# A convolution in far and near parts, and a 1x1 output product as three float32r products

## The reference

```python
xn = group_norm(x)                                  # 32 groups, no scale or shift
f  = relu(Wc @ xn + bc)                             # 1x1, 256 -> 64 channels
g  = relu(mean_hw(xn) @ Wc.T + bc)                  # 64 values
g_kern = g * Wkk + bkk                              # 64 x 3 x 3
sk = relu(Wc @ max_over_3x3_blocks(xn) + bc)        # 64 x 3 x 3
dynW = relu(Wck[:, 0] * g_kern + Wck[:, 1] * sk + bck)   # out 64 x in 64 x 3 x 3
y  = conv3x3(f, dynW, pad=1) + b_ad                 # another kernel for each image
out = x + Wf @ y + bf                               # 1x1, 64 -> 256 channels
```

## Time and profile before

| | |
|---|---|
| time, median of 3 runs | 511.19 us |
| lowest, highest | 509.42, 512.63 us |
| span of the profiled execution | 507.5 us |
| PE, PEld busy | 487.8, 383.7 us |
| DVE, ACT, POOL busy | 418.9, 426.6, 296.2 us |
| DMA | 158.01 MB, 311 GB/s |

### The profile page before, as it was taken

How to read it: one execution, slowest core, us unless ns; L and a number is a source line. 1 busy time by engine, 2 the same in 40 slices (tenths; PEclk the granted TensorE clock), 3 DMA queues, 4 the chain that set the end, 5 groups by cost and what they waited for, 6 DMA issues and landing times.

```text
span 507.5 us, 19231 instructions
## 1 busy us (share of the span) xinstructions
PE 487.8 (96%) x8349; PEld 383.7 (76%) x8349; DVE 418.9 (83%) x653; ACT 426.6 (84%) x486; POOL 296.2 (58%) x231
## 2 busy tenths in 40 slices
PE   5989999999999999999999999999999999999993
PEld 2454664677788888888888978888887878888781
DVE  6978879988888889888888988888889887888544
ACT  5779999998999999999999899999999989995231
POOL 5224586555577655556775555577655556765543
PEclk9999999999999999999999999999999999999997
DMA  8945778999898998998999999989999998953467
GB/s 335 418 134 201 265 283 289 366 353 349 323 333 334 323 332 340 348 359 293 320 362 333 333 365 343 318 297 360 307 366 334 341 333 298 361 208 145 185 270 296
DMA packets 48868, 158.01 MB, mean 311 GB/s; under 512 B 4752, under 2 KB 15888, under 8 KB 48784
## 3 DMA queue, kind: packets, MB, share of 16 engines
q1 hardware_dynamic: 34096, 93.07, 54.0%
q10 hardware_dynamic: 14688, 63.70, 31.0%
HBM read 75.94 MB, written 75.50 MB: 298 GB/s over the span
## 4 chain that ended last, share of the span: by engine, by line
PE 81%; ACT 2%; DVE 0%; issue 0%; DVEq 0%; ACTq 0%
PE ps L1129 30%; PE ps L1260 23%; PE ps L1228 21%; PE ps L1179 7%; ACT unused L609 1%; DVE X L859 0%; ACT unused L596 0%; ACT f_hi L688 0%; DVEq L153 0%; ACT f L694 0%; ACT Y L586 0%; PE ps L1372 0%; ACT dyn_b L709 0%; ACT dyn_hi L707 0%; ACTq L130 0%
## 5 line engine op out<-in xcount | busy, mean ns | idle before, releaser
L859 DVE SCALAR_TENSOR_TENSOR X<-ps,out_bias,X 128x960 f32<-128x960 f32 (+1 forms) x189 | 185.2, 1008 | 17.1 <-PE ps L1260 16.8
L1260 PE MATMUL ps<-Y,const 64*64 64x480 f32 (+1 forms) x1536 | 165.1, 486 | 0.0
L596 ACT ACTIVATE unused<-X,neg_mean 128x2304 bf16<-128x2304 f32 x60 | 132.0, 2201 | 0.4 <-DVE neg_mean L998 0.4
L512 POOL TENSOR_TENSOR dyn_a<-const,pool_g 128x576 f32<-128x576 f32 x30 | 34.9, 1165 | 163.8 <-DVE pool_g L883 163.8
L609 ACT ACTIVATE unused<-X 128x2304 bf16<-128x2304 f32 x60 | 126.9, 2115 | 0.0
L1228 PE MATMUL ps<-X,wcn_t 64*64 64x384 f32 (+1 forms) x1296 | 115.5, 486 | 0.7 <-issue 0.7
L935 DVE TENSOR_REDUCE feats<-X 128x6 f32<-128x1536 f32 x64 | 111.6, 1744 | 0.0
L1228 PEld LDWEIGHTS ps<-X,wcn_t 64*64 64x64 f32 x1296 | 82.0, 133 | 29.8 <-issue 7.4
L1260 PEld LDWEIGHTS ps<-Y,const 64*64 64x64 f32 x1536 | 78.2, 133 | 7.5 <-issue 2.8
L527 POOL TENSOR_TENSOR f_lo<-f,f_hi 128x1152 f16<-128x1152 f32 x32 | 71.4, 2232 | 19.5 <-ACT f L694 19.5
L1129 PE MATMUL ps<-f_hi,dyn_hi 64*64 64x480 f16 x1152 | 69.0, 365 | 2.5 <-ACT dyn_hi L715 1.1
(11 more groups left out here) (101 smaller groups left out, 541.8 us busy)
## 6 DMA issues: line engine op xcount, KB each, us to landing
X<-x SPq DMA_DIRECT2D x63, 1152.0 KB, 9.5
out<-X ACTq DMA_DIRECT2D x54, 1152.0 KB, 9.7
out<-X SPq DMA_DIRECT2D x7, 1152.0 KB, 8.0
out<-X SPq DMA_DIRECT2D x6, 480.0 KB, 3.5
stack<-f_hi SPq DMA_DIRECT2D x64, 32.5 KB, 2.5
stack<-f_lo SPq DMA_DIRECT2D x64, 32.5 KB, 5.4
X<-x SPq DMA_DIRECT2D x2, 576.0 KB, 7.1
upper<-f_hi SPq DMA_DIRECT2D x32, 32.5 KB, 3.5
```

Source lines behind the costliest of these rows:

```text
L596: nc.scalar.activation(unused[:, t], pixels(u, t), ACT.Square, scale=1.0 / SIDE, bias=neg_mean[:, n % 2, 1:2], accum_out=feats[:, (n + 1) ...
L859: nc.vector.scalar_tensor_tensor(out=out, in0=unit_psum(piece, bank, col), scalar=out_bias[:, t:t + 1], in1=out, op0=ALU.add, op1=ALU.add) ...
L1260: mm = nc.tensor.matmul(ps[rows, bank + q, col:col + width], wft[lanes, t, rows], Y[lanes, n % 2, at:at + width], start=True, stop=True)
```

## The change

The convolution no longer has a rest with stacked rows. Each block of 24 rows is done as 7 + 7 far rows and 5 + 5 near rows, near and far from the seam between the blocks: `conv(n, FAR, term)` has products of 336 columns, `conv(n, NEAR, term)` of 240, both three terms of 36 products of 64*64. One row on each side of the seam is copied by DMA (`halo`) instead of five rows three or two times.

y leaves PSUM as two float32r tensors: ACT writes the rounded Y_hi, DVE writes Y_lo as the difference. The output weights are split the same way once. A unit is three float32r products (hi x hi, hi weights x lo, lo weights x hi), each for both blocks, with 64 rows and 128 columns of the array (64*128). `project_f` is the 128*64 form in every image, now 512, 512 and 139 columns wide. The gains move from DVE to ACT, the rounding of the dynamic weights from ACT to POOL, two Newton steps from DVE to POOL, and all stores from ACT's queue to SP's. PSUM banks are dealt anew, and all lists of calls are in another order.

```diff
--- before.py
+++ after.py
...
-MAIN_ROWS = 10
-MAIN = MAIN_ROWS * SIDE
-REST_ROWS = HROWS - 2 * MAIN_ROWS
-REST = REST_ROWS * SIDE
-STACK_ROWS = 2 * (REST_ROWS + 1)
...
+FAR, NEAR = 0, 1
+ROWS = (7, 5)
+PART = tuple(rows * SIDE for rows in ROWS)
+FIRST = (((0, 7), (10, 17)), ((14, 19), (0, 5)))
...
+NEAR_BANK = 4
+NEAR_AT = 256
...
+CHUNKS = ((0, 512), (512, 512), (1024, 128))
...
+OUT_UNITS = ((0, 0), (0, 1), (1, 0), (1, 1), (0, 2), (1, 2))
+UNITS = len(OUT_UNITS)
+PIECES = ((0, PART[FAR]), (PART[FAR], PART[FAR]), (2 * PART[FAR], PART[NEAR]))
+UNIT_BANKS = (2, 6, 6, 6, 2, 6)
+PENULT_BANKS = (2, 6, 2, 6, 2, 6)
+LAST_BANKS = (2, 6, 0, 2, 6, 0)
+PENULT_AIDED = (5,)
...
+            def halo(f, ready, arrived, n):
+                if inside(n):
+                    sp.wait_ge(*ready)
+                    sp.dma_start(f[CM:P, n % 2, 0:1, :], f[0:CM, n % 2, HROWS:HROWS + 1, :]) \
+                        .then_inc(arrived[n % 2], 16)
+                    sp.dma_start(f[0:CM, n % 2, HROWS + 1:HROWS + 2, :], f[CM:P, n % 2, 1:2, :]) \
+                        .then_inc(arrived[n % 2], 16)
...
+            for i in range(1, N - 1):
+                load(i + AHEAD, 0)
+                seam_low(i)
+                load(i + AHEAD, 1)
+                seam_high(i + 1)
+                store(i - 1, 0)
+                store(i - 1, 1)
...
+                nc.gpsimd.tensor_scalar(wf_hi[:], wft[:], 1.0, 1.0, ALU.mult, ALU.mult).then_inc(wf_step, 1)
+                pool.wait_ge(wf_step, 2)
+                nc.gpsimd.tensor_tensor(wf_lo[:], wft[:], wf_hi[:].bitcast(F32), ALU.subtract) \
...
+                nc.gpsimd.tensor_scalar(dyn_a[:], per_gain[:], mean_act[:, n % 2, MEAN:MEAN + 1], 1.0,
+                                        ALU.mult, ALU.mult).then_inc(dyn_step, 1)
...
+            def weights_high(n):
+                if inside(n):
+                    pool.wait_ge(dyn_step, count(n - SUMS, SUM_STEPS, SUM_STEPS))
+                    pool.wait_ge(conv_mm[NEAR], count(n, -1))
+                    nc.gpsimd.tensor_scalar(dyn_hi[:, n % 2], dyn_a[:], MOST, 0.0, ALU.min, ALU.max) \
+                        .then_inc(dyn_hi_ready, 1)
...
-            def y_main_out(n):
-                u, lap = n % RING, n // RING
-                if inside(n):
-                    act.wait_ge(main_mm, count(n, 1))
-                    nc.scalar.activation(Y[:, n % 2, 0:2 * MAIN].rearrange("p (b f) -> p b f", b=2),
-                                         ps[:, 0:2, 0:MAIN], ACT.Identity).then_inc(y_main, 1)
+                act.wait_ge(squares, halves_done(N - 1, 1))
...
+            def y_high_out(n, part):
+                if inside(n):
+                    act.wait_ge(conv_mm[part], count(n, 1))
+                    nc.scalar.activation(part_y(Y_hi, part), part_psum(part), ACT.Identity) \
+                        .then_inc(y_high[part], 1)
...
+                proj = ps_flat[:, HPIX:HPIX + FEATS]
+                nc.vector.tensor_scalar(f_bias[:, n % 2:n % 2 + 1], proj[:, NEG:NEG + 1], bcs[:], None, ALU.add)
+                nc.vector.tensor_scalar(mean_act[:, n % 2], proj[:, 0:TAPS + 1], bcs[:], 0.0,
+                                        ALU.add, ALU.max).then_inc(relu_ready, 1)
...
-            def y_rest_out(n):
-                u, lap = n % RING, n // RING
-                if inside(n):
-                    dve.wait_ge(rest_mm, count(n, 1))
-                    both = ps[:, rest_bank(n):rest_bank(n) + 2, 0:REST].rearrange("p q f -> p f q")
-                    nc.vector.tensor_reduce(Y[:, n % 2, 2 * MAIN:HPIX], both, AX.X, ALU.add).then_inc(y_rest, 1)
...
+            def y_low_out(n, part):
+                if inside(n):
+                    dve.wait_ge(conv_mm[part], count(n, 1))
+                    dve.wait_ge(y_high[part], count(n, 1))
+                    nc.vector.tensor_tensor(part_y(Y_lo, part), part_psum(part), part_y(Y_hi, part).bitcast(F32),
+                                            ALU.subtract).then_inc(y_low[part], 1)
...
+            def conv(n, part, term):
+                pe_terms = ((dyn_hi, f_hi), (dyn_lo, f_hi), (dyn_hi, f_lo))
+                order = (0, 2, 1) if n < SUMS else (0, 1, 2)
+                w, f = pe_terms[term]
                 if term == 0:
                     pe.wait_ge(f_evac, count(n, 1, 2))
                     pe.wait_ge(dyn_hi_ready, highs_done(n, 0))
...
+                    wait(pe, y_high[part], n)
+                    wait(pe, y_low[part], n)
+                    if part == NEAR:
+                        pe.wait_ge(halo_hi[n % 2], 32 * (n // 2 + 1))
+                        pe.wait_ge(f_evac, count(min(n + 2, N), 0, 2))
+                        ahead = 2 if n < EARLY else 3
+                        pe.wait_ge(var_ready, min(n + ahead, N))
+                        pe.wait_ge(neg_ready, min(n + ahead + 1, N))
+                elif term == 1:
...
+                        r = FIRST[part][q][h] + dy
+                        bank, at = (q, 0) if part == FAR else (NEAR_BANK + q, NEAR_AT)
                         mm = nc.tensor.matmul(
...
+                            ps[CM * h:CM * (h + 1), bank, at:at + PART[part]],
                             w[lanes, n % 2, tap, :],
...
+                at, width = CHUNKS[c]
+                column = at
+                if c == len(CHUNKS) - 1:
+                    wait(pe, y_low[NEAR], n, -1)
+                if c == len(CHUNKS) - 1 and n >= SUMS:
+                    width += FEATS
                     pe.wait_ge(feats_read, count(n, 1))
                 for t in range(HALVES):
                     for h in range(2):
...
+                        src = half(n % RING, t) + HPAD * h + at
+                        mm = nc.tensor.matmul(ps_flat[CM * h:CM * (h + 1), column:column + width],
+                                              wcn_t[:, n % 2, t, :], X[:, src:src + width],
                                               start=(t == 0), stop=(t == HALVES - 1))
                 mm.then_inc(f_mm, 1)
...
                 mm.then_inc(feats_mm, 1)
-            def product(n, k, t, piece, bank, col):
-                at, width, _ = PIECES[piece]
-                for q, h in ((0, 0), (1, 1), (0, 1), (1, 0)):
-                    lanes, rows = (slice(CM * tile, CM * (tile + 1)) for tile in (q, h))
-                    mm = nc.tensor.matmul(ps[rows, bank + q, col:col + width], wft[lanes, t, rows],
-                                          Y[lanes, n % 2, at:at + width],
-                                          start=True, stop=True)
+            terms = ((wf_hi, Y_hi), (wf_hi, Y_lo), (wf_lo, Y_hi))
+            def product(n, k):
+                t, piece = OUT_UNITS[k]
+                at, width = PIECES[piece]
+                bank = unit_bank(n, k)
+                for s, (w, y) in enumerate(terms):
+                    for h in range(2):
+                        lanes = slice(CM * h, CM * (h + 1))
+                        mm = nc.tensor.matmul(ps[:, bank + h, 0:width], w[lanes, t, :], y[lanes, at:at + width],
+                                              start=(s == 0), stop=(s == len(terms) - 1))
                 mm.then_inc(out_mm, 1)
+            def products_near(n):
...
+            def products_near(n):
+                for turn in range(2):
+                    for k in (4, 5):
+                        t, piece = OUT_UNITS[k]
+                        at, width = PIECES[piece]
+                        bank = unit_bank(n, k)
+                        for s, (w, y) in enumerate(terms):
+                            for h in range(2):
+                                lanes = slice(CM * h, CM * (h + 1))
+                                side = (turn + h) % 2
+                                if turn == 1 and s == 0:
+                                    pe.wait_ge(handed[1 - h], count(n, k - 3, 2))
+                                mm = nc.tensor.matmul(ps[:, bank + side, h * width:(h + 1) * width], w[lanes, t, :],
+                                                      y[lanes, at + side * width:at + (side + 1) * width],
+                                                      start=(s == 0), stop=(s == len(terms) - 1))
+                                if turn == 0 and s == len(terms) - 1:
+                                    mm.then_inc(handed[h], 1)
+                        if turn == 1:
+                            mm.then_inc(out_mm, 1)
             def unit(k, n):
...
+                conv(i, FAR, 0)
+                unit(1, i - 1)
+                if i > TURN:
+                    project_f(i + 1)
+                    unit(2, i - 1)
+                    conv(i, FAR, 1)
+                    group_sums(i + 2)
+                    unit(3, i - 1)
+                    conv(i, FAR, 2)
+                else:
                     if i < EARLY:
...
+                units_near(i - 1)
+                conv(i, NEAR, 0)
+                conv(i, NEAR, 2 if i < SUMS else 1)
+                conv(i, NEAR, 1 if i < SUMS else 2)
+                unit(0, i)
```

(66 more changed lines are left out.)

808 lines of the change are left out of this document (310 added, 498 removed).

## The result

The changed kernel takes **580.38 us** (median of 4 runs, 579.44 to 582.07) against 510.31 for the kernel before on the same chip (507.68 to 512.63). The ratio is 1.138, with a 95% interval of 1.133 to 1.143. The direction was forecast (chance 57%), the size was not: 536, with a range up to 551.

The account below looks back on a forecast made before the run. TensorE, full at 14.62 us an image, was taken as the bound: 13.9 plus 1.6 for ten form changes gives 15.5, +0.88 over 27 images, plus 1 for start and end, 536 us; own range 515 to 550, with rivals 496 to 551.

Parts of the forecast that it names:

- TensorE's own work: TensorE's list in a steady image: 13.9 us plus 1.6 for form changes, 15.5 against 14.62.
- A float32r product is one pass: Units: one pass at one column a cycle, 0.1456 us a far step; units -0.80 us an image; rival of slower passes 4%.
- A near unit's step: Near units: 12 steps of 240 columns, each held by a 128-column weight load at 0.111 us, 1.33 us together.
- A change of form costs 0.16 us: TensorE's steady list: ten changes of array form an image, each waiting for an empty array, +1.6 us.
- the forecast's 13.9 us of the rest: Steady image on TensorE net of convolution +0.07, projection 0 and units -0.80 us, before changes of form.
- The rival with 28%: Changes between 64-row forms free, only the projection's two pay: 14.2 us an image, 500 us in all; chance 28%.
- Hidden by TensorE: Steady image: DVE 12.7, ACT 12.9, POOL at most 13.5 us, all under 15.5, so each costs nothing.
- idle rows released by ACT, DVE or DMA: Sign in the profile after: such idle rows on PE would mean the cover of the other engines failed.
- The first three images ... and the end ...: +1: Start and end of the run: first images already pay one pair and wait for ACT, end one longer image; +1 us.
- the prediction's own bounds: Whole run: form changes at 0.10 to 0.20 us, with a load of 0.05 in five, give 515 to 550 us.
- One queue for all big transfers: SP's DMA queue: rival that a late load makes ACT and DVE wait each image, some 560 us; chance 3%.
- its bound: POOL (GpSimd) in a steady image: three tensor_scalar of 576 elements, priced from a 1.65 us row, at most 13.5 us.

Follow-up runs that it names:

- experiment 1: Changed kernel with unit 3 moved ahead of the second outer maxima in VectorE's steady list: 555.96 us, ratio 1.091 to the kernel before.
- experiment 3: Changed kernel, unit 3 ahead of the maxima, each unit one float32 product in four 64*64 tiles, low parts left out: 548.14 us, ratio 1.076.
- experiment 2: Kernel before with only each unit's product run as two float32 products of 64 rows and 128 columns instead of four of 64*64: 544.89 us, ratio 1.070.
- experiment 7: Changed kernel with unit 3 ahead of the maxima, start reordered, and image 0's unit 0 in banks 6 and 7: 551.72 us, ratio 1.078.
- Experiment 8: Kernel of experiment 7 plus nine idle products on TensorE between image 0's unit 0 and image 1's far convolution: 548.95 us, ratio 1.077.

## Why the prediction was wrong, step by step

**TensorE's own work: right.** Forecast 15.5 us an image; measured 15.5 beside the wait, and 15.53 in experiment 1 without it.
- A float32r product is one pass: 0.15 or 0.16 us for a pair of 336 columns, each with one weight load (forecast 0.1456).
- A near unit's step is 0.114 us (forecast 0.111, from the earlier trace rows) behind a first one of 0.19: 303.20, 303.39, and ten more steps to 304.53. In the list of weight loads each load of 128 columns starts with the product before its own, and its own starts 0.11 us later, so the loads hold the pace, as assumed.
- Near terms take 0.94 to 0.96 us (forecast 0.95). Far terms took 1.30 without a change behind them (experiment 3; forecast 1.31).
- A change of form costs 0.16 us, as read from the earlier trace rows: 0.16 by experiment 2, 0.17 by experiment 3, and (15.53 - 13.9) / 10 = 0.16 by experiment 1, if the forecast's 13.9 us of the rest is taken as right. The rule cited from the Trainium skill, TensorEngine Tiling (Array Packing), Key Properties, that a change of the tiling mode drains the engine, agrees with the overlap of 0.07 us at every edge of experiment 2. The rival with 28%, free changes between forms of 64 rows, falls by the same run.

**"Hidden by TensorE": the step that failed.** The prediction summed each engine's work (DVE 12.7, ACT 12.9, POOL at most 13.5, all under 15.5) and costed them at nothing. The sums were right: 12.62, 12.98 and 10.44 measured. But a sum under the image's length doesn't hide a result that stands in the wrong place of its engine's list. The new banks made TensorE's near units wait for unit 3's addition, and VectorE had a reduction of 1.74 us ahead of it: 1.02 us in each of 27 images, some 27 us (25.5 of them idle by the profile), of which moving one line gave 24.4 back. The prediction named this row as what would show it wrong ("idle rows released by ACT, DVE or DMA"), but put no chance on it. It was foreseeable: the order of the lists was at hand, and the wait for unit 3 in `units_near` with the maxima ahead of `unit(3, i - 1)` stands in it. I checked what each engine had to do and not where each awaited result stood.

**"The first three images ... and the end ...: +1": failed too.** The start lost 23.3 us up to image 5, the end 2.4. Of the 23.3, some 4 are TensorE's own 0.8 to 0.9 an image and 1 is the wait of the steady images, in image 4 already. By the windows of the five images TensorE was idle for 18.5 of 102.9 us, before for 4.7 of 80.0, so 14 of the 23 are waits. What the runs show of the rest:
- Image 0's near part waited for image 1's f, and ScalarE's four channel means stood ahead of f of image 3. Reordering both took 3.9 us off the time.
- ScalarE's passes bound image 3: about 4 us of its 22 went when squares were cut.
- Single waits for f in the shared banks remain; taking the longest away alone moved no time (experiment 7).
- The clock, for which the prediction had no term. In the changed kernel the near terms of image 0 took 1.8 us each at the low level in place of 0.95, after an idle stretch of 3.6 us. Experiment 8 shows this link on image 1. Three stretches of these images stand at the low level, each at a wait of 2.5 to 3.6 us; TensorE was busy for 15.6 us in them, so by an estimate the clock cost at most half of that, 7.8 us:

```profile
39.38 2.01 PE L1116 MATMUL ps<-f_hi,dyn_hi 64*64 64x240 f16 x36 [3.64 <-ACT dyn_hi L689]
41.16 2.04 PE L1116 MATMUL ps<-f_lo,dyn_hi 64*64 64x240 f16 x36
```

```profile
38.42:45.25 6.83, 5.87 (x110) 5.54 (x112) 1.30 (x2) 1.74 (x4) 3.46 (x2) 0.50 0.76 223
79.38:86.21 6.83, 6.28 (x96) 5.81 (x100) 3.11 (x3) 3.11 (x4) 5.28 (x5) 0.50 0.29 112
103.27:106.69 3.42, 3.42 (x40) 3.16 (x44) 2.01 (x3) 3.42 (x5) 3.25 (x4) 0.50 0.04 7
```

How the 23 us divide exactly stays open, because these causes feed each other and the start's time moves by some microseconds from run to run. Nor do the prediction's own bounds follow from its sum: ten changes at 0.10 and at 0.20 with 0.05 more in five give 520 and 554 us, not 515 and 550. The result lies above both.

**The other rivals.** One queue for all big transfers did no harm: in the steady stretch no engine waited for a DMA, and the DMA share fell from 1.00 to 0.78. GpSimd was cheaper than its bound: its tensor_scalar of 576 elements with two multiplying operands took 0.74 us and the min-max pair 0.67, against the 1.65 of the earlier trace rows, a row with one operation. Nothing hung on it.

## What to carry to other kernels

Where a change gives banks or buffers to another user, write down for each new wait which instruction ends it and what stands ahead of that instruction in its engine's list. An engine that idles a quarter of its time can still be late by the length of one reduction. And where all of TensorE's work has one array form, price a new form by its edges, two for each place where it appears: here three passes for four saved 0.80 us an image by the prediction's sum, and ten edges cost 1.6.

## What was not expected of the hardware

- A stall can hide the emptying of the array at the change next to it. Counted from the end of streaming the wait was 1.12 us, and taking it out gained 1.01.
- The low level of the clock outlasts the wait that brought it. Behind 2.3 us of idle time in experiment 7, terms and units ran at 1.2 GHz for about 6 us (43.9 to 50, granted clock 0.50), and nine idle products, which TensorE had time for, kept it at 2.4 GHz.
- Gaps of up to 1.6 us that no engine's result ends stood on TensorE in experiment 3 (ten, 5.3 us together), whose images have 312 products instead of 294. Whether the number of products makes them isn't shown.
